# A relational graph convolution with a gated update: three products whole instead of one, the edge table and the row sums earlier

## The reference

```python
h = max(layernorm(x), 0)
u = h @ root + bias
for r in range(8):
    mask = (edge_type == r)
    sums = segment_sum(h[src] * mask[:, None], dst, 1250)
    cnt  = segment_sum(mask, dst, 1250)
    u = u + (sums / max(cnt, 1)[:, None]) @ weight[r]
z = concat([u, h], axis=1) @ w_gate + b_gate
out = x + tanh(u) * z + h * (1 - z)
```

## Time and profile before

| | us |
|---|---|
| median of three runs | 1606.29 |
| the profiled execution | 1619.65 |
| its span, first to last instruction | 1617.9 |
| PE busy (products 1084.1, one-hot sums 212.6) | 1303.7 |
| VectorE busy | 992.7 |
| GpSimd busy | 884.7 |
| ScalarE busy | 447.7 |

### The profile page before, as it was taken

One profiled execution on the slowest core, in us unless ns is written; L12 is line 12 of the kernel. 1 busy time (PEld: TensorE's weight loads), 2 busy tenths in 40 slices (PEclk: granted clock), 3 DMA queues, 4 the chain that ended last, 5 costly groups with the idle time before them and its releaser, 6 DMA issues.

```text
span 1617.9 us, 20012 instructions
## 1 busy us (share of the span) xinstructions
PE 1303.7 (81%) x6045; PEld 648.0 (40%) x6045; DVE 992.7 (61%) x1276; ACT 447.7 (28%) x592; POOL 884.7 (55%) x1060
## 2 busy tenths in 40 slices
PE   3879666489998996289889889988989877668697
PEld 1434222134443443044444444444444444334364
DVE  6664488787765753265566545646647655645676
ACT  5353322533233432131322222223304122213000
POOL 2258837544887778566476657654745565531000
PEclk9989887799999998599999999989999989779899
DMA  5641002113424233167757565657688566653876
GB/s 192 205 144 49 12 33 91 64 57 93 136 84 117 64 112 84 25 198 228 228 163 234 195 194 175 212 178 221 208 259 250 150 213 195 204 176 108 214 209 183
DMA packets 125024, 248.89 MB, mean 154 GB/s; under 512 B 20246, under 2 KB 60749, under 8 KB 124940
## 3 DMA queue, kind: packets, MB, share of 16 engines
q1 hardware_dynamic: 92124, 165.39, 32.2%
q0 software_dynamic: 32816, 82.39, 18.3%
HBM read 189.22 MB, written 77.05 MB: 165 GB/s over the span
## 4 chain that ended last, share of the span: by engine, by line
POOL 27%; DMA 25%; PE 18%; issue 13%; DVE 10%; ACT 4%; SPq 2%; POOLq 1%; DVEq 0%; ACTq 0%
DMA early<-y_rows,idx 19%; POOL table_rows L608 14%; PE ps L1292 13%; PE ps L1253 4%; DMA out_dram<-hT 3%; DVE W L923 2%; POOL onehot L645 2%; POOL early L582 2%; ACT early L752 2%; POOL early L637 1%; DMA early<-u_rows 1%; DVE early L994 1%; DMA hT<-u_rows 1%; POOL dcol L626 1%; POOL idx L627 1%
## 5 line engine op out<-in xcount | busy, mean ns | idle before, releaser
L1292 PE MATMUL ps<-W,hT 128*128 128x512 f16 (+1 forms) x4740 | 1084.1, 390 | 113.7 <-DVE W L923 63.6
L1292 PEld LDWEIGHTS ps<-W,hT 128*128 128x128 f16 (+1 forms) x4740 | 487.9, 104 | 670.4 <-issue 104.8
L1253 PE MATMUL ps<-early,onehot 128*125 x768 | 212.6, 413 | 110.3 <-POOL onehot L645 69.6
L637 POOL DMA_INDIRECT early<-y_rows,idx x192 | 230.1, 1198 | 92.9 <-PE ps L1256 41.2
L608 POOL DMA_INDIRECT table_rows<-edge_src,early x160 | 226.0, 1412 | 82.3 <-issue 82.3
L645 POOL TENSOR_SCALAR onehot<-iota_d,dcol 128x125 f16<-128x125 f16 x186 | 151.5, 815 | 207.4 <-DMA early<-y_rows,idx 202.0
L777 ACT ACTIVATE yhl<-W 128x512 f16<-128x512 f32 x140 | 87.5, 627 | 510.1 <-DVE W L1048 315.0
L923 DVE SCALAR_TENSOR_TENSOR W<-W,wsc 128x2048 f16<-128x2048 f32 x71 | 176.6, 2491 | 40.6 <-ACT W L714 37.9
L1253 PEld LDWEIGHTS ps<-early,onehot 128*125 x768 | 105.3, 144 | 177.6 <-issue 137.1
L714 ACT ACTIVATE W<-W,wsc 128x2048 f16<-128x2048 f32 x71 | 140.1, 1989 | 49.5 <-DVE W L939 31.2
L1023 DVE TENSOR_TENSOR yhl<-W,yhl 128x512 f16<-128x512 f32 x140 | 114.1, 815 | 14.2 <-ACT yhl L777 13.8
(11 more groups left out here) (170 smaller groups left out, 827.5 us busy)
## 6 DMA issues: line engine op xcount, KB each, us to landing
y_rows<-yhl SPq DMA_DIRECT2D x144, 256.0 KB
W<-in_L_gnn_weight_dram SPq DMA_DIRECT2D x32, 1024.0 KB
early<-u_rows SPq DMA_DIRECT2D x30, 448.0 KB
u_rows<-early SPq DMA_DIRECT2D x30, 448.0 KB
...
```

Source lines behind the costliest of these rows:

```text
L637: pool.indirect_dma_start(out=G[:, b, :], out_offset=None, in_=y_rows[i], in_offset=bass.IndirectOffsetOnAxis(ap=idx[:, b, :], axis=0), bo ...
L1253: nc.tensor.matmul(ps[0:DT, 4 + half, :], hot_t, rows[:, bass.ds(ring_slot * (2 * D) + (part * D + half * HC), HC)], start=first and part ...
L1292: last = nc.tensor.matmul(ps[0:rows, n % 4, :], hT[:, m, v_h, k, n0:n0 + rows], Wh[:, MAT[w][c], v_w, k, :], start=(first and v_h + v_w == ...
```

## The change

Seven things change together.

1. rel0, rel1 and root are plain products (`PLAIN = 3`). rel1 and root run all ten row tiles for the left half of the columns and then for the right half. There are 325 units; rel2 starts at unit 60, gate_h at 270, gate_u at 305. root is evacuated by one VectorE instruction a unit.
2. One array of 80 x 160 counts replaces the chunks. VectorE makes the one-hot and one running count for 20 groups at a time, at units 5, 9, 13 and 15. Factors of one, with a zero at each group's start, are set by GpSimd. The totals come from the last column.
3. In units 21 to 28 VectorE makes 80 instructions of 125x160, one for each group (`rank`). In units 29 to 32 it sums them by quarters of the edges and makes positions (`positions`). GpSimd scatters each quarter as it is ready. The clearing of the ring is ahead of the scatters. ScalarE and GpSimd have no part in the ranks.
4. The sums of h's blocks are made on VectorE in units 41 to 55, behind the positions.
5. The row sums go in four sweeps: relations 0 to 2, 3 and 4, 5 and 6, and 7 (30, 20, 20 and 10 groups), from unit 102 on. The u rows make one more trip to HBM and back.
6. The table is unpacked three units ahead of the first group, at 99, where it was eight ahead, at 156.
7. A row of y holds left half (high, low) and then right half (high, low), so a store writes runs of 2 KB where it wrote runs of 1 KB. A gather still takes one row of 4 KB.

The core of the diff:

```diff
-    SWEEPS = [(0, 4), (4, 6), (6, 8)]
+    SWEEPS = [(0, 3), (3, 5), (5, 7), (7, 8)]
...
     PH = 7
-    FIRST = [0] + [2 * NJ + PH * HT * (w - 1) for w in range(1, NW)]
+    PLAIN = 3
+    FIRST = [2 * NJ * w if w <= PLAIN else 2 * NJ * PLAIN + PH * HT * (w - PLAIN) for w in range(NW)]
     NU = FIRST[W_GU] + 2 * NJ
-    ORDER0 = [(j, h) for j in range(7) for h in range(2)] + [(j, 0) for j in range(7, NJ)] + [(j, 1) for j in range(7, NJ)]
+    ORDER = [[(j, h) for j in range(7) for h in range(2)] + [(j, 0) for j in range(7, NJ)] + [(j, 1) for j in range(7, NJ)],
+             [(j, h) for h in range(2) for j in range(NJ)], [(j, h) for h in range(2) for j in range(NJ)]]
...
-    AGG_AT = ([164 + g * 86 // 40 for g in range(40)] + [250 + g * 52 // 20 for g in range(20)]
-              + [305 + g * 26 // 20 for g in range(20)])
+    AGG_AT = ([102 + g * 63 // 30 for g in range(30)] + [168 + g * 68 // 20 for g in range(20)]
+              + [238 + g * 34 // 20 for g in range(20)] + [273 + g * 28 // 10 for g in range(10)])
...
-    TURN_U = {STEP_END[FINAL + j] + 4: j for j in range(NJ)}
+    TURN_U = {}
+    for j in range(NJ):
+        freed = phase_end(W_GH, 1 if j < HT else 3)
...
     NORM_AT = {0: 2, 1: 3, 3: 4, 5: 5, 7: 6, 8: 7, 10: 8, 12: 9}
     TURN_AT = {1: 2, 3: 3, 5: 4, 7: 5, 9: 6, 10: 7, 12: 8, 14: 9}
-    S_HIGH_AT = {10: 0, 13: 1, 16: 2, 18: 3, 20: 4}
-
-
-    HOT8_AT = {3: 0, 4: 1, 6: 2, 9: 3, 11: 4}
-    BEHIND_LOW = {7: [("sums", 0)], 8: [("low", 0), ("sums", 1)],
-                  9: [("low", 1), ("sums", 2), ("low", 2), ("sums", 3), ("low", 3), ("sums", 4), ("low", 4)]}
+
+    S_AT = {41 + 3 * i: i for i in range(HT)}
+    S_HIGH_AT = {42 + 3 * i: i for i in range(HT)}
+    S_LOW_AT = {43 + 3 * i: i for i in range(HT)}
+
+    SQ = 4
+    KEYS_AT, SCAN_AT, TOTALS_AT, BOUNDS_AT = 2, {5: 0, 9: 1, 13: 2, 15: 3}, 17, 19
+    RANK_AT = {21 + i: range(10 * i, 10 * i + 10) for i in range(8)}
+    POSITIONS_AT = {29 + i: i for i in range(SQ)}
+    TABLE_AT = AGG_AT[0] - 3
...
-
-    CONV_AT = {0: [], 1: [17, 18, 21, 22, 31, 36, 41], W_GU: [FIRST[W_GU] + d for d in (-5, -3, -2, -1)]}
-    SUM_AT = {1: [19, 20, 23, 26]}
-    PEEK_AT = {1: [(5, 2), (6, 0), (7, 1), (9, 3)]}
-    SCALE_AT = {1: 10}
-    for w in range(2, NW):
+        return 4 * w + c if w < PLAIN else 4 * PLAIN + 7 * (w - PLAIN) + c
+
+
+    LAND_AT = {2: [(1, 2)], 3: [(1, 0)], 4: [(1, 1)], 5: [(1, 3)],
+               26: [(2, q) for q in range(4)], 46: [(3, q) for q in range(4)]}
+
+
+    CONV_AT = {0: [], 1: [17, 18, 22, 24], 2: [35, 36, 42, 44], W_GU: [FIRST[W_GU] + d for d in (-5, -3, -2, -1)]}
+    SUM_AT = {3: [FIRST[3] + d for d in (-1, 0, 4, 8)]}
+    PEEK_AT = {1: [(5, 2), (6, 0), (7, 1), (9, 3)], 2: [(28 + q, q) for q in range(4)], 3: [(48 + q, q) for q in range(4)]}
+    SCALE_AT = {1: 10, 2: 32, 3: 52}
+    for w in range(PLAIN, NW):
         if w < W_GU:
-            CONV_AT[w] = [FIRST[w] + d for d in (-5, -3, 2, 6, 11, 16, 21)]
-            SUM_AT[w] = [FIRST[w] + d for d in (0, 1, 4, 8)]
-        PEEK_AT[w] = [(FIRST[w - 1] + d, q) for q, d in enumerate((19, 21, 24, 25))]
...
                     m0 = (REL[w] - SWEEPS[i][0]) * N + n0
-                    sp.dma_start(y_rows[i][m0:m0 + rows, :].rearrange("n (v c m) -> n v c m", v=2, c=2)[:, :, c, :],
+                    sp.dma_start(y_rows[i][m0:m0 + rows, c * D:(c + 1) * D].rearrange("n (v m) -> n v m", v=2),
...
+            def scan_factors(b):
+                g0, g1 = b * NG // SQ, (b + 1) * NG // SQ
+                pool.memset(scan3[:, g0:g1, 1:EC], 1.0).then_inc(s["factors_ready"], 1)
+                pool.memset(scan3[:, g0:g1, 0:1], 0.0).then_inc(s["factors_ready"], 1)
...
-
-            pool.wait_ge(s["table_filled"], 16)
-            pool.wait_ge(s["pos_ready"], 1)
-            for c in range(EC):
-                pool.indirect_dma_start(out=table_rows, out_offset=bass.IndirectOffsetOnAxis(ap=at_i[:, c:c + 1], axis=0),
-                                        in_=packed[0:EP, c:c + 1], in_offset=None).then_inc(s[f"scattered{c // (EC // SQ)}"], 16)
+                if 2 <= i <= SQ + 1:
+                    scan_factors(i - 2)
+
+            pool.wait_ge(s["lnT_hi"], NJ)
+            pool.wait_ge(s["lnT_lo"], NJ)
+            for b in range(2):
+                pool.wait_ge(s[f"hs_stored{b}"], 16 * NJ // 2)
             pool.memset(early[:, 0:4 * D], 0.0).then_inc(s["ring_clear"], 1)
             pool.memset(onehot[:, 0, 0:2], 0.0).then_inc(s["onehot_free"], RING)
             pool.memset(onehot[:, 1, 0:2], 0.0).then_inc(s["tile_ready"], RING)
+
+            pool.wait_ge(s["table_filled"], 16)
+            for c in range(EC):
...
             def high_sums(i):
                 act.wait_ge(s["s_added"], i + 1)
+                act.wait_ge(s["pos_ready"], SQ)
                 nc.scalar.activation(hT[:, S2:S4 + 1, 0, :, cols(i)], sbuf_s, ACT.Copy).then_inc(s["s_high"], 1)
...
+                    dve.wait_ge(s["lnT_lo"], NJ)
+                else:
+                    dve.wait_ge(s["s_low"], i)
+                step(nc.vector.tensor_tensor(a4, h(A21, 0), h(A21, 1), ALU.add))
+                nc.vector.tensor_tensor(a1, h(A22, 0), a4, ALU.add).then_inc(s["dve_step"], 1)
+                steps[0] += 1
+                step(nc.vector.tensor_tensor(a3, h(A11, 0), a4, ALU.subtract))
+                nc.vector.tensor_tensor(a1, a1, h(A22, 1), ALU.add).then_inc(s["dve_step"], 1)
+                steps[0] += 1
+                step(nc.vector.tensor_tensor(a3, a3, h(A11, 1), ALU.add))
+                step(nc.vector.tensor_tensor(a2, a1, h(A11, 0), ALU.subtract))
+                step(nc.vector.tensor_tensor(a2, a2, h(A11, 1), ALU.subtract))
+                step(nc.vector.tensor_tensor(a4, h(A12, 0), a2, ALU.subtract))
...
+            def low_sums(i):
+                dve.wait_ge(s["s_high"], i + 1)
+                nc.vector.tensor_tensor(hT[:, S2:S4 + 1, 1, :, cols(i)], sbuf_s, hT[:, S2:S4 + 1, 0, :, cols(i)],
+                                        ALU.subtract).then_inc(s["s_low"], 1)
...
+            def scan_part(b):
+
+                g0, g1 = b * NG // SQ, (b + 1) * NG // SQ
+                step(nc.vector.tensor_tensor(hot3[:, g0:g1, :], key[0:EP, :].unsqueeze(1).to_broadcast([EP, g1 - g0, EC]),
+                                             iota_g[0:EP, g0:g1].unsqueeze(2).to_broadcast([EP, g1 - g0, EC]), ALU.is_equal,
+                                             saturate=False))
+                dve.wait_ge(s["factors_ready"], 2 * (b + 1))
+                part = scan[:, g0 * EC:g1 * EC]
+                nc.vector.tensor_tensor_scan(out=part, data0=part, data1=hot[:, g0 * EC:g1 * EC], initial=0.0,
+                                             op0=ALU.mult, op1=ALU.add).then_inc(s["scan_ready"], 1)
+
+            def rank(groups_of):
+                dve.wait_ge(s["scan_ready"], SQ)
+                for g in groups_of:
+                    nc.vector.scalar_tensor_tensor(out=pos3[:, g, :], in0=scan3[:, g, :], scalar=tb[0:EP, g:g + 1],
+                                                   in1=hot3[:, g, :], op0=ALU.add, op1=ALU.mult).then_inc(s["ranked"], 1)
+
+            def positions(b):
+
+                q = slice(b * EC // SQ, (b + 1) * EC // SQ)
+                dve.wait_ge(s["ranked"], NG)
+                dve.wait_ge(s["table_filled"], 16)
+                step(nc.vector.tensor_reduce(pos[:, q], pos3[:, :, q].rearrange("p g c -> p c g"), AX.X, ALU.add))
+                step(nc.vector.tensor_scalar(hi_t[:, q], pos[:, q], -(P - 1) / 2, 1.0 / P, ALU.add, ALU.mult))
+                step(nc.vector.tensor_scalar(hi_t[:, q], hi_t[:, q], ROUND, None, ALU.add))
+                step(nc.vector.tensor_scalar(hi_t[:, q], hi_t[:, q], -ROUND, None, ALU.add))
+                step(nc.vector.scalar_tensor_tensor(out=at_f[:, q], in0=hi_t[:, q], scalar=-float(P), in1=pos[:, q],
+                                                    op0=ALU.mult, op1=ALU.add))
+                nc.vector.scalar_tensor_tensor(out=at_i[:, q], in0=at_f[:, q], scalar=float(TMAX), in1=hi_t[:, q], op0=ALU.mult,
                                                op1=ALU.add).then_inc(s["pos_ready"], 1)
...
+                if w == W_ROOT:
+                    half = out_place(o)[2]
+                    rows = LT[out_place(o)[1]][1]
+                    dve.wait_ge(s["gemm_done"], n + 1)
+                    dve.wait_ge(s["brow_loaded"], 16)
+                    dve.wait_ge(s[f"y_stored{o % 4}"], 16 * (o // 4))
+                    nc.vector.scalar_tensor_tensor(out=yf[0:rows, o % 4, :], in0=part[0:rows], scalar=wscale(w, 1)[0:rows],
+                                                   in1=brow[0:rows, half * HC:(half + 1) * HC], op0=ALU.mult,
+                                                   op1=ALU.add).then_inc(s[YDONE], 1)
+                    return
...
-                                         rows[:, bass.ds(ring_slot * (2 * D) + (part * D + half * HC), HC)],
```

(6 more changed lines are left out.)

316 lines of the change are left out of this document (114 added, 202 removed).

## The result

The changed kernel took 1518.65, 1518.93, 1521.82 and 1522.23 us, a median of 1520.38 us, beside 1610.92 us of the kernel before (four runs, 1605.07 to 1616.33). The ratio is 0.944, with a 95% interval of 0.939 to 0.948: 90.5 us less. The forecast was 1534 in a range of 1458 to 1590. A second group of runs on another occasion gave a ratio of 0.939 (0.933 to 0.944).

What follows compares the result with a forecast made beforehand. PE was taken as the busiest engine, with waits at the second product, table and row sums. 532 to the sums, 892 for them and 122 for the end gave 1546 against 1617.9; 1606 - 72 = 1534 us, range 1458 to 1590.

Steps and rivals of the forecast that it cites:

- Products: PE's matmuls over the whole kernel: 120 more at 0.2235 us each, 27 us of added PE work.
- First product: Start of the kernel: four scans replace ten passes, 13.5 us more on VectorE; +2 us taken, ending at 170 us.
- Units 20 to 59: rel1 and root as plain units on PE: 40 x 5.4 = 216, and 6 for two weight maxima: 222 us.
- rival 2: VectorE bounds units 20 to 60; 45 to 55 us come back, giving about 1585 us; chance 0.12.
- Table: GpSimd's scatters, then unpack and gather: first scatter at 233 us, last at 523, first tile at 537, formerly 698.4.
- The 290: Time in us for GpSimd's 160 scatters, taken between 285 at the old rate and 296 priced by VectorE's two-operand time.
- Rival 4: VectorE's work holds the scatters up: gain gone at 2.26 us a scatter, 1692 us at 2.8; chance 0.06.
- Sweeps 1 and 3: Row sums paced by gathers at 3.82 us a tile: 288 us for the first, 188 for the third.
- Sweep 2: Row sums with 70 units and 48 tiles, PE-bound: the old 203 us plus 18 more units, 251 us.
- Sweep 4: Last row sums, 24 tiles in 32 units: 87 + 30 + 15 + 8 and 25 of waits, 165 us.
- Rival 1: In the row sums gathers keep up with PE, stores being out of the way: 1458 us; chance 0.14.
- Rival 3: The u rows come late in more sweeps: 56 us more, 1590 us; chance 0.08.

Runs made afterwards that it cites:

- The rank steps twice: The changed kernel with each of VectorE's 80 rank steps preceded by a copy of itself into scratch, with a wait behind it: 1547.58 us, ratio 0.959.
- the late kernel: The changed kernel with its first sweep (30 groups) started at unit 132 in place of 102 and pressed into 33 units: 1572.32 us, ratio 0.972.

## Why the prediction was right, by its own steps

- **Products.** 120 matmuls were to cost 27 us. The group of products grew by 16.8 us, from 1084.1 to 1100.9:

```profile
L1272 PE MATMUL ps<-W,hT 128*128 128x512 f16 (+2 forms) x4860 | 1100.9, 387 | 24.4 <-DVE W L900 23.3
...
L1233 PE MATMUL ps<-early,onehot 128*125 x768 | 208.4, 409 | 107.4 <-POOL onehot L605 97.3
```

  The other 10 us came back in the clock, granted at 0.947 of full on average against 0.919. The stretch of the old second product stood at 0.81, and 421 product matmuls took 103.3 us there, 0.245 each; units 20 to 59 now stand at 0.98, and 953 took 208.3 us, 0.219 each. The prediction had no term for that.
- **First product.** +2 forecast, +3.5 measured (171.9 for 168.4). VectorE went from 83.65 to 97.09 us busy, the 13.5 that were booked.
- **Units 20 to 59.** 222 forecast, 218.6 measured. VectorE was not the bound; rival 2 fell. The rank steps twice show how near it was: of the 37 us added, 25 reached the first scatter and the end.
- **Table.** 537 forecast, 524.0 measured. 7 us were before the first scatter, 7 in the scatters. The 290 was a compromise between 285 by rate and 296 by two-operand time; the measured 282.7 lies below both. The price by time (0.57, measured 0.47 for long steps) was applied to h's sums, most of which are too short to matter: that term was mis-sized, 24 us where the timelines show about 10, and where taking the sums away gave 1.3. Rival 4, with 2.26 us a scatter to lose the gain and 2.8 for its price, was far off: the scatters took 282.7 / 160 = 1.77.
- **Sweeps 1 and 3.** 288 and 188 forecast, 288 and 193 measured. That 288 fits to the microsecond is luck. From the start of the stretch to the issue of the 72nd gather it is 263 us, where 72 tiles at 3.82 had been booked at 275; from there to 807 it is 25, where five units had been booked at 13. In that gap GpSimd stands for 21.05 us, until the last y of sweep 2's relations is stored (timeline line below), and again for 20.25 us ahead of sweep 3: a sweep can't begin before its products are stored, whatever the gathers do. The prediction allowed for that only by its five units and by 5 us to get going. And the pace was taken as the gathers' own, where the late kernel shows 3.46 us a tile. GpSimd's first copy of sweep 2, then PE's one-hot group and GpSimd's in sweeps 1 and 2:

```profile
807.15 2.33 POOL L586 COPY dcol<-edge_dst 128x1 f32 x1 [21.05 <-DMA y_rows<-yhl]
...
L1233 PE MATMUL ps<-early,onehot 128*125 x480 | 126.9, 403 | 56.5 <-POOL onehot L605 55.8 <-issue 0.6
...
L605 POOL TENSOR_SCALAR onehot<-iota_d,dcol 128x125 f16<-128x125 f16 x116 | 102.6, 884 | 127.1 <-DMA early<-y_rows,idx 124.7 <-issue 0.2
```

- **Sweep 2.** 251 forecast, 243 measured. PE's busy time grew by 39.8 us (188.7 to 228.4) and its idle time hardly (14.3 to 14.6), so the error is in the price of the added work. The stretches hold 641 and 841 product matmuls, which is 16.7 units more and not 18, at 2.4 us each and not 2.7. The prices 2.71 a unit and 1.24 a tile count an overlap twice: for the old sweep 2 they give 52 x 2.71 + 48 x 1.24 = 200, and PE was busy for 188.7.
- **Sweep 4.** 165 forecast, 153 measured. Of the 12 us, 8 lie in PE's work (131.7 busy, where 87 + 30 + 15 + 8 = 140 had been booked by the same prices) and 4 in its waits (21.5 for 25). In 1243 to 1397 us PE's groups:

```profile
L1233 PE MATMUL ps<-early,onehot 128*125 x95 | 28.3, 443 | 7.4 <-DVE early L1101 3.2 <-POOL onehot L605 3.0 <-issue 1.2
...
L1265 PE MATMUL ps<-ident_h,W 125*128 125x125 f16 x160 | 12.9, 227 | 9.4 <-ACT hT L750 5.2 <-DVE W L1117 3.0 <-issue 1.1
```

  Waits for the add fell from 29.8 to 3.2 us; 10 were booked. Waits for one-hots fell from 18.4 to 3.0. The other waits came to 18.3 us, where 15 had been booked.
- **Rival 1**, the gathers keeping up, did not happen, and the row layout has no part in the gain that these runs can tell. **Rival 3**, late u rows, did not either: in all four sweeps PE waited 5.3 us for the add, so the extra trip cost next to nothing. The 9 us for one uncovered load stand in no row and were not needed.

The forecast was 72 us and the result 90.5. Between the spans it is 101, so the sum was off by 29: 13 us at the table, 12 in sweep 4, 8 in sweep 2 and 1 at the end, less 5 in sweep 3. The time, 1534 against 1520, is off by only 14, and that is luck: the prediction carried over the 13 us by which the profiled execution of before stood above its median, and in the changed kernel that execution stood 2 below.
